# Weight residuals tied to VectorE's finish, and routed rows scattered to token order

## The reference

```python
xn = layernorm(x)                                  # x: 8 x 512 x 256
out = x + attention(xn, k, v) + ffn(xn)

def attention(q, k, v):                            # k, v: 1024 x 256
    scale = q[:, ::128].reshape(8, -1)             # one factor per key, of the batch's own rows
    return softmax((q @ k.T) * scale[:, None, :]) @ v

def ffn(x):                                        # 4096 tokens of 256
    shared = gelu(x @ Wfc_s + bfc_s) @ Wproj_s + bproj_s
    top2 of softmax(x @ Wr) over 8 experts, gates renormalised to sum 1
    routed = sum of gate_e * (gelu(x @ Wfc[e] + bfc[e]) @ Wproj[e] + bproj[e]) over the two
    return shared + routed
```

## Time and profile before

| | us |
|---|---|
| median of 3 runs | 867.32 (866.02 to 872.22) |
| the profiled execution | 861.36 |
| its span in the trace | 859.5 |
| PE busy | 785.8 (91% of the span) |
| DVE busy | 490.7 (57%) |
| ACT busy | 441.0 (51%) |
| POOL busy | 257.3 (30%) |
| mean granted TensorE clock | 0.972 |

### The profile page before, as it was taken

The page is one execution under the profiler, slowest core; times in us unless marked ns, Lnnn a source line. Parts: engine busy times, 40 slices in busy tenths (PEclk is TensorE's granted clock), DMA queues, the critical chain, the costliest instruction groups (busy, mean ns, idle before and its releaser), DMA issues.

```text
span 859.5 us, 20915 instructions
## 1 busy us (share of the span) xinstructions
PE 785.8 (91%) x7222; PEld 661.5 (77%) x7222; DVE 490.7 (57%) x1144; ACT 441.0 (51%) x845; POOL 257.3 (30%) x318
## 2 busy tenths in 40 slices
PE   4888899699969899999999999999999999977893
PEld 3777776476647677999999989999999998865772
DVE  6888868888898776444434453333333333353464
ACT  6665466365636544565465555555555555524350
POOL 5666756557655730000000000000000000263655
PEclk9999999899979999999999999999999999996997
DMA  9464341647464535344322554454545452142334
GB/s 307 157 221 135 137 168 54 233 154 233 142 221 153 197 118 185 124 165 153 123 68 97 158 183 161 158 160 146 172 135 175 128 186 86 45 125 74 119 119 134
DMA packets 70379, 129.11 MB, mean 150 GB/s; under 512 B 12248, under 2 KB 56480, under 8 KB 63920
## 3 DMA queue, kind: packets, MB, share of 16 engines
q1 hardware_dynamic: 64176, 111.57, 39.3%
q0 software_dynamic: 6144, 16.79, 6.1%
HBM read 88.29 MB, written 40.04 MB: 149 GB/s over the span
## 4 chain that ended last, share of the span: by engine, by line
PE 69%; DVE 15%; issue 6%; POOL 4%; ACT 2%; DMA 2%; another core or an unknown queue 2%; DVEq 0%; SPq 0%; POOLq 0%; ACTq 0%
PE ps_h L1266 28%; PE ps_v L1286 27%; PE ps_v L1406 6%; PE ps_h L1338 4%; DVE xn L844 3%; PE ps_t L1202 2%; DVE prob L968 2%; POOL w_split L609 2%; PE ps_t L1352 1%; DVE p_t L982 1%; POOL y_rows L666 1%; DVE acc L1171 1%; DVE h_split L893 1%; ACT h L693 1%
## 5 line engine op out<-in xcount | busy, mean ns | idle before, releaser
L893 DVE TENSOR_TENSOR h_split<-h,h_split 128x512 f16<-128x512 f32 (+1 forms) x224 | 144.8, 655 | 164.0 <-ACT h_split L699 160.9
L693 ACT ACTIVATE h<-ps_h,b_fc 128x256 f32<-128x256 f32 (+1 forms) x320 | 125.9, 444 | 170.9 <-PE ps_h L1266 170.9
L666 POOL DMA_INDIRECT y_rows<-slots_y,y_row_all x64 | 64.4, 1007 | 480.9 <-DMA slots_y<-prob 437.8
L1266 PE MATMUL ps_h<-x_t,w_split 128*128 128x256 f16 (+1 forms) x1920 | 193.3, 261 | 0.0
L1286 PE MATMUL ps_v<-w_stage,h_split 128*128 128x256 f16 x1704 | 192.6, 273 | 0.0
L1266 PEld LDWEIGHTS ps_h<-x_t,w_split 128*128 128x128 f16 x1920 | 170.5, 98 | 17.0
L1286 PEld LDWEIGHTS ps_v<-w_stage,h_split 128*128 128x128 f16 x1704 | 165.1, 98 | 18.4
L699 ACT CAST h_split<-h 128x512 f16<-128x512 f32 (+1 forms) x224 | 131.1, 585 | 10.4 <-ACT h L693 0.4
L1266 PE MATMUL ps_h<-x_t,w_shared 128*128 128x256 f16 x768 | 94.0, 278 | 13.4 <-issue 13.0
L693 ACT ACTIVATE h<-ps_h,b_t 128x256 f32<-128x256 f32 x128 | 53.5, 468 | 99.6 <-PE ps_h L1266 58.1
L1266 PEld LDWEIGHTS ps_h<-x_t,w_shared 128*128 128x128 f16 x768 | 75.0, 99 | 29.4 <-issue 19.8
(11 more groups left out here) (153 smaller groups left out, 624.4 us busy)
## 6 DMA issues: line engine op xcount, KB each, us to landing
w_split<-wpack SPq DMA_DIRECT2D x17, 1024.0 KB, 5.1
w_stage<-wpack SPq DMA_DIRECT2D x17, 1024.0 KB, 5.0
wpack<-w_split SPq DMA_DIRECT2D x16, 1024.0 KB, 5.1
w_stage<-in_L_ffn_Wfc_dram SPq DMA_DIRECT2D x8, 1024.0 KB
w_stage<-in_L_ffn_Wproj_dram SPq DMA_DIRECT2D x8, 1024.0 KB
x_split<-slots_x SPq DMA_DIRECT2D x31, 256.0 KB, 3.5
slots_y<-prob SPq DMA_DIRECT2D x31, 256.0 KB, 3.2
b_pj<-in_L_ffn_bproj_dram SPq DMA_DIRECT2D x40, 128.0 KB, 3.1
```

What stands on the lines that cost most here:

```text
L666: g.indirect_dma_start(y_rows[:, n, kk, :], None, slots_y, bass.IndirectOffsetOnAxis(ap=y_row_all[:, c:c + 1], axis=0)).then_inc(s_gat[n], 16)
L693: ins = nc.scalar.activation(h32[:, hc, 0:n], ps_h[:, hc * TILE:hc * TILE + n], ACT.Gelu_apprx_tanh, bias=bias[:, hc:hc + 1], scale=1.0 / WS)
L893: ve.tensor_tensor(h_split[par][:, 1, 2 * b:2 * b + 2, 0:n], h32[:, 2 * b:2 * b + 2, 0:n], h_split[par][:, 0, 2 * b:2 * b + 2, 0:n], ALU.s ...
L1266: ins = mm(ps_h[:, hc * TILE:hc * TILE + cols], wv[:, wl, c, hc * P:(hc + 1) * P], x[:, xl * DC + c, 0:cols], start=n == 0, stop=n == 3 * ...
```

## The change

**Weight preparation.** All 16 jobs move into the attention, in four buffers instead of two: the two `w_stage` and `w_split`, and the buffers of `y_rows`, `h32` and the two `h_split`, which are free there. A job is one piece of work every two steps up to job 9; jobs 10 to 15 start at u = 20, 21, 22, 24, 25 and 26, with scale and cast in the same step (`scale_slot`, `hi_slot`) and POOL's two residual pieces two steps later (`lo_slot`). A residual piece is one instruction over 1024 columns, and it waits until DVE's `finish` of step u - 2 is done. DVE's `scale_scores` moves ahead of the normalising and splitting in its step. The 16 `add_bias` leave their places and stand in a row on POOL after the last `finish`.

**Routed rows.** A slot row grows from 1024 to 1032 bytes: POOL writes the token's first expert and twice its number behind the row (`x_split` tail). In a routed step DVE keeps the tail (`keep_tail`) and computes the target row (`rows_of`), and POOL scatters each 128 result rows straight to `tokens_y`, where a token's two rows lie side by side (`scatter_y`, one scatter at a time). `store_slots`, the table `y_row_all` with its nine DVE instructions, and the 64 gathers go. In the last stage SP loads each block's pair of rows with one plain DMA (`load_y`), blocks 16 to 31 first (`LATE`).

```diff
+ROWX = ROW + 4
-        def job_of(i):
-            return 2 + i // 2 if i % 2 == 1 and i < NA else None
+        SLOW = 10
+        def scale_slot(n):
+            return 2 * n if n < SLOW else 2 * SLOW + (n - SLOW) + (n - SLOW) // 3
+        def hi_slot(n):
+            return 2 * n + 1 if n < SLOW else scale_slot(n)
+        def lo_slot(n, half):
+            return 2 * n + 2 + half if n < SLOW else scale_slot(n) + 2
+        LATE = list(range(NA * SUB, QT)) + list(range(NA * SUB))
...
 @block.sync
             for u in range(QT):
...
-                if u % 2 == 0:
-                    m = JOB_B + u // 2
-                    if m <= JOBS:
-                        store_job(m - 1)
-                    if m + 1 < JOBS:
-                        load_job(m + 1)
+                if u == 0:
+                    load_job(3)
+                for n in range(JOBS):
+                    if u == lo_slot(n, 1) + 1:
+                        store_job(n)
+                        if n + 4 < JOBS:
+                            load_job(n + 4)
...
             def load_slots(j, par, half, first=False):
                 if not first:
                     wait_ge(sp, s_tr2, j - 1)
+                    wait_ge(sp, s_tail, j - 1)
...
-            for par in range(2):
-                wait_ge(sp, s_w_out[par], 16 * EXPERTS)
+            for n in range(4):
+                wait_ge(sp, s_w_out[n], 16 * (JOBS // 4))
             wait_ge(sp, s_bt_out, 16)
             wait_ge(sp, s_table, TABLE)
             load_fc(0, 0, first=True)
...
+            wait_ge(sp, s_y_out, scattered(ROUTED, 0, False))
+            for p in range(GATHERS):
+                load_y(p)
...
 @block.gpsimd
             def split_w_lo(m, piece):
...
-                for at in range(piece * 1024, piece * 1024 + 1024, 256):
-                    ins = g.tensor_tensor(dst[:, 2048 + at:2304 + at], w_stage[par][:, at:at + 256], dst[:, at:at + 256],
-                                          ALU.subtract)
-                ins.then_inc(s_wlo, 1)
+                at = piece * 1024
+                g.tensor_tensor(dst[:, 2048 + at:3072 + at], src[:, at:at + 1024], dst[:, at:at + 1024],
+                                ALU.subtract).then_inc(s_wlo, 1)
...
             for u in range(QT):
...
+                for n in range(JOBS):
+                    for half in range(2):
+                        if u == lo_slot(n, half):
+                            wait_ge(pool, s_fin, u - 1)
+                            split_w_lo(n + 2, half)
+                if phase == 2 and i - 1 < SHARED:
+                    scatter(i - 1)
+            wait_ge(pool, s_bpj_in, 16)
+            wait_ge(pool, s_fin, QT)
+            for i in range(SHARED):
+                add_bias(i)
+            def scatter_y(j, par, mixed=False, first=False):
+                wait_ge(pool, s_to, j + 1)
+                wait_ge(pool, s_ev, 2 * (R0 + j) + 2)
+                for a in range(1 if mixed and par else SUB):
+                    if not first or a:
+                        wait_ge(pool, s_y_out, scattered(j, par, mixed) + 16 * a)
+                    g.indirect_dma_start(tokens_y, bass.IndirectOffsetOnAxis(ap=to_i[par][:, a:a + 1], axis=0),
+                                         y_sb[par][:, a, :], None).then_inc(s_y_out, 16)
...
 @block.vector
+            def rows_of(j, par, half=False, mixed=False):
+                subs = 1 if half else SUB
+                dve.wait_ge(s_bpjx_in[par], nth(j, par))
+                dve.wait_ge(s_tail, j + 1)
+                if not (isinstance(j, int) and j < 2):
+                    dve.wait_ge(s_y_out, scattered(j - 1, 1 - par, mixed))
+                ve.scalar_tensor_tensor(out=to_i[par][:, 0:subs], in0=tail[par][:, 0:subs, 0], scalar=b_pj[par][:, D:D + 1],
+                                        in1=tail[par][:, 0:subs, 1], op0=ALU.not_equal, op1=ALU.add).then_inc(s_to, 1)
...
             def body2(j, par, prev=False, this=False, following=False, mixed=True):
                 split_h(R0 + j, par, n, banks=(0, 1, 2))
+                rows_of(j - 1, 1 - par, prev, mixed)
                 copy_slots(j + 1, 1 - par, n=P if following else TILE)
```

More of the change, by code:

```diff
@@ L123, in moe_attention_block @@
         xn = sb2("xn", [P, SUB, D], f32)
-        x_split = [sb(f"x_split{n}", [P, SUB, ROW], f16) for n in range(3)]
+        x_split = [sb(f"x_split{n}", [P, SUB, ROWX], f16) for n in range(3)]
         wr32 = sb("wr32", [P, DC, EXPERTS], f32)
@@ L523, in _, with body2 @@
             load_slots(2, 0, is_half(2))
-            def body2(j, par, slots=None, out=None):
+            def body2(j, par, slots=None):
                 if j is not LAST:
@@ L615, in scatter @@
                 wait_ge(pool, s_rb, (i + 1) * RB)
+                for a in range(SUB):
+                    end = x_split[i % 3][:, a, ROW:].bitcast(f32)
+                    g.tensor_copy(end[:, 0:1], exp_all[:, (i * SUB + a) * TOP:(i * SUB + a) * TOP + 1]).then_inc(s_row_tail, 1)
+                    g.tensor_copy(end[:, 1:2], token_2[:, i * SUB + a:i * SUB + a + 1]).then_inc(s_row_tail, 1)
+                wait_ge(pool, s_row_tail, 2 * SUB * (i + 1))
                 for a in range(SUB):
@@ L629, in _ @@
             split_w_lo(1, 1)
-            add_bias(0)
             for i in range(1, NA):
@@ L658, in _ @@
[L658 to L668 removed]
+                if phase == 0 and i < SHARED:
+                    inv_std(i)
@@ L671, in _ @@
+            scatter_y(0, 0, True, first=True)
+            scatter_y(1, 1, True)
+            with pairs(pool, 2, MIXED) as j:
+                scatter_y(j, 0, True)
+                scatter_y(j + 1, 1, True)
+            with pairs(pool, MIXED, ROUTED) as j:
+                scatter_y(j, 0)
+                scatter_y(j + 1, 1)
         @block.scalar
@@ L1068, in tables, with keep_tail @@
                     glink(ve.tensor_tensor(gates[:, :, 1], gap_exp[:, :], gates[:, :, 0], ALU.mult))
+            def keep_tail(par, subs=SUB):
+                ve.tensor_copy(tail[par][:, 0:subs, :], x_split[par][:, 0:subs, ROW:].bitcast(f32)).then_inc(s_tail, 1)
             def copy_first(bank):
@@ L1085, in _ @@
                 p_lo(u)
+                if u + 2 < QT:
+                    scale_scores(u + 2)
                 if phase == 0 and i < SHARED:
@@ L1110, in evict @@
             def evict(t, par, bias, subs=SUB, first=False):
-                if not first:
-                    dve.wait_ge(s_y_out[par], (t - R0 - par) * 8)
                 for a in range(subs):
@@ L1179, in _ @@
                     evict2(ROUTED - 1, 1)
+                    dve.wait_ge(s_bias, SHARED)
                 else:
+                    if i > NA + 1:
+                        dve.wait_ge(s_gated, TOP * PER * (i - NA - 1))
                     evict_shared(i - 1, t - 1)
-                    for u in range((i - NA - 1) * per, (i - NA) * per):
-                        add_routed(u)
-            for u in range(QT - per, QT):
-                add_routed(u)
+                    dve.wait_ge(s_ev, 2 * t)
+                    for p in range((i - NA - 1) * PER, (i - NA) * PER):
+                        add_routed(p)
+            for p in range(QT - PER, QT):
+                add_routed(p)
             dve.wait_ge(s_gated, 2 * QT)
```

272 lines of the change are left out of this document (129 added, 143 removed).

## The result

The changed kernel takes **822.2 us** (median of 4 runs, 821.8 to 822.7) where the kernel before, timed beside it, takes 866.7 (4 runs, 862.8 to 872.2): a ratio of 0.948, 95% interval 0.943 to 0.954. The profiled execution is one of 822.5 us. Predicted were 832.3 us in a range of 815 to 854.

What follows compares the result with a forecast made beforehand. PE, busy 91% of the span, was taken as the bound, with only its idle time to win. Terms -8 - 20 + 10 + 13 + 0 - 30 = -35 us took the 867.3 us median to 832.3, range 815 to 854.

Steps and rivals of the forecast that it cites:

- First stage: Stage before the attention: without 8 bias adds and four jobs PE waits less for DVE, -8 us (-11 to -4).
- Attention, middle: PE's five waits for DVE's `finish` and the clock's dip go, less some late pieces: -20 us (-24 to -10).
- second rival: Attention: residual pieces still hold DVE and the waits only move, gaining 2 us instead of 20: 850 us, 12%.
- Attention, end: First routed loads wait behind the last job's store, so PE's slot transposes come late: +10 us (+6 to +13).
- Start of the routed steps: Sixteen bias adds in a row on POOL delay the first scatters and hold DVE: +13 us (3 to 22).
- The milder case: Start of routed steps: each DVE instruction gets in after one add, adds stretch, PE's wait becomes about 10 us.
- Steady routed steps: Later routed steps: DVE's two small instructions and POOL's scatters fit within each step, 0 us, bound +5.
- third rival: Routed steps: slow scatters one after the other let POOL set the pace, +73 us, 905 us, 5%.
- Last stage: Without POOL's gathers PE's "issue" gaps go and the tail shortens: -30 us (-34 to -12).
- first rival: Last stage: PE's gaps come from long written-out code beside DMA traffic, not the gathers; 854 us, 14%.

Runs made afterwards that it cites:

- the order and the tie: Kernel before with DVE's `scale_scores` ahead of norm and split (860.9 us), then also POOL's residual pieces waiting for DVE's `finish` of the q tile before (857.2 us).
- The run with early loads: Changed kernel with SP issuing the first two slot loads and `load_fc(0)` at u == 28, ahead of the last stores of split weights: 809.2 us.
- spreading the adds: Changed kernel with one bias add behind each of the first sixteen routed steps' scatters instead of sixteen in a row: 817.7 us.
- the order in DVE's step: Changed kernel with early loads, spread adds and eight y buffers, plus `rows_of` and `keep_tail` moved behind the `x_t` copy: 799.1 us.
- eight buffers: Changed kernel with eight buffers instead of four for the last stage's y loads, the other four in the keys' tile: 820.6 us.

## Why the prediction was right, term by term

**First stage: -8 predicted, -10.6 measured.** PE's idle time there went from 9.3 us to 3.0 by the windows, close to the 7 taken. The clock gave more than the 1 us taken: from the same event on, some 850 matmuls take 81.3 us instead of 84.6, at a granted clock of 1.00 instead of 0.97. No run took this apart; that the adds and the four jobs held DVE rests on the two traces alone.

**Attention, middle: -20, measured -20.3.** Waits and clock went as reckoned: idle time from 19.9 us to 3.6, busy time from 198.8 to 194.8. But the two means that I named, the order and the tie, gave only 11.3 us in the kernel before; what the other 9.0 hang on is open. My sentence that "single pieces are over before `xn` comes" was wrong in detail: POOL is often late behind its row scatter, and in the step at 160 us a piece and the norm meet:

```profile
160.05 2.13 POOL L646 TENSOR_TENSOR h_split<-y_rows,h_split 128x1024 f16<-128x1024 f32 x1
```

```profile
160.10 2.55 DVE L895 TENSOR_SCALAR xn<-acc,mean_var,rstd 128x256 f32<-128x256 f32 x2 [0.17 <-POOL rstd L632]
```

One piece then costs DVE under 2 us, not the 9 of two runs of eight pieces and an add, and the scores' product is already ahead of it; PE waited 0.7 us at most for `finish`. The second rival (residuals still in the way, 850) falls with the middle's 20.3 us.

**Attention, end: +10, measured +11.3**, with 9.2 us of waiting and the clock's dip, by the chain I described, link by link: residual 2.14, store 4.29, slots 3.96. The 9.2 us of waiting were reckoned at 8.6, and the clock took 2.4 where I had up to 2. The run with early loads won 13.0 and so confirms the cause.

**Start of the routed steps: +13, measured +11.2.** Of the two ways of colliding it was the milder: each DVE instruction got in behind one add. The Trainium skill's rule in SBUF — State Buffer, "SBUF: two separate sides", that the port pair is held for one instruction, fits these rows, the 22.95 us of sixteen adds and the 1.5 us of an `h_split`; the row of 9.56 us still doesn't. That 13 and 11.2 lie close is in part luck. The milder case had one wait of about 10 us at step 4, behind late scatters, with adds stretched by 7 us. They stretched by 2.5, and there were three waits of PE (1.77, 2.93 and 2.62 us), at steps 2, 3 and 4, 7.3 us together; the other 3.9 us, which the term didn't hold, are PE's busy time (391.58 us against 387.70 for the same 3895 matmuls), at a granted clock down to 0.83 between 358 and 365 us. Only the third wait ends with a scatter. In the other two DVE's own row numbers and tails, lengthened by the adds, stood ahead of `x_t`. Those I had put into the steady steps at 0.2 us each and "nothing". For that reason spreading the adds won 4.5 and not 8 to 11, and the order in DVE's step won the rest (4.4).

**Steady routed steps: 0.** Right: 387.8 us without adds against 387.7 before. The third rival (scatters set the pace, 905) needed 5.5 us each. Some are that slow: 20 of the 71 took over 5 us from issue to landing, up to 6.5. But they are not the rule, and PE never waited for them in the steady steps; the median was 3.6 us, in the changed kernel's DMA issues:

```profile
tokens_y<-prob,to_i POOLq DMA_INDIRECT x71, 3.6
```

(The prediction has it that before's trace holds no such scatter next to 1 MB loads. The 64 row scatters to `slots_x` are there, in the stages with the jobs' loads; what the trace lacks is their time to landing.)

**Last stage: -30, measured -30.5**, 25.6 of gaps and 4.9 of the tail. For the tail the prediction's times give 6.4 us (12.7 to 6.3); the "-9" in its first rival is too much by them. It had the loads four blocks ahead and so out of the way, but one of 4.45 us stood in the chain at the end, and eight buffers took it out. The first rival (gaps of another cause) is refuted by the gathers put back, 78.9 us of loss, against none for the same bytes by plain loads. In Runtime: NRT & Kernel Launch, "Instruction fetch mechanics", the Trainium skill has the fetching of instructions run ahead and mostly hidden. Beside plain loads PE had no gap, which agrees; beside back-to-back gathers PE stood 63.5 us marked "issue", and no run shows whether fetching was what held it.

**The sum.** -38.9 us instead of -35 leaves 6 of the 10 us between 832.3 and 822.2 open. They come from the last step: I took it that the profiled execution would stay 6 us below the median. That gap was the spread of before, whose runs reach from 862.8 to 872.2; the changed kernel's four lie within 1 us, and its profiled execution is at its median.

## What to carry to other kernels

Where a program's longest idle time is marked "issue", look at what another engine's queue is doing some 8 us earlier; a run of indirect DMAs without waits between them cost PE here more than any dependence, and arranging the data so that a plain load does cost PE nothing. Letting each land first cost PE nothing either, but 64 of them then took 224 us instead of 80. Before hiding side work on an engine that holds up another, find the one instruction that the bottleneck engine waits for, and put every small one behind it: then sixteen adds, one per step, were free. A load that needs only half of what has been stored should wait for that half.

## What the hardware did that I had not expected

Sixty-four indirect gathers 1.25 us apart brought PE from some 9 matmuls per us to 51 in 79 us, with rows of 64 bytes much as with rows of 1 KB, from 8 or 9 us behind their start to some 9 us behind their end, and took the granted clock to 0.51. One at a time, 3.6 us apart in the mean over all 64, they cost nothing. And DVE under a row of POOL's adds was held for one add per instruction here, where under two runs of POOL's 256-wide pieces with an add between them one `xn` was held for 9.2 us, twice in before's trace. It is not the code alone that decides: in the run with the order and the tie the first stage is before's, and there a `mask_sum` of 0.16 us once took 6.62, as long as an add and eight pieces:

```profile
33.24 6.62 DVE L883 TENSOR_TENSOR mask_sum<-mask_sum,mask 128x8 f16<-128x8 f16 x1
33.57 1.28 POOL L600 TENSOR_TENSOR acc<-acc,b_pj_s 128x512 f32<-128x512 f32 x1
34.80 5.04 POOL L609 TENSOR_TENSOR w_split<-w_stage,w_split 128x256 f16<-128x256 f32 x8
```

What decides stayed open.
